# Sums of phi(k) v as four 32 by 33 products on TensorE's column groups instead of one of 128 by 129

## The reference

```
qkv = conv1x1(x); agg = conv1x1_grouped(conv5x5_depthwise(qkv))
ms  = concat([qkv, agg]) -> 64 heads of (q, k, v), each 8 dims, 4096 positions
q, k = relu(q), relu(k);  v = [v, 1]            # 9th column of ones
kv  = einsum('bgnd,bgne->bgde', k, v)            # per head: 8 x 9, summed over n
out = einsum('bgnd,bgde->bgne', q, kv)
out = out[..., :-1] / (out[..., -1:] + 1e-15);  return conv1x1(out)
```

## Time and profile before

| | |
|---|---|
| median of 3 runs | 9206.59 us (9197.57 to 9220.26) |
| the profiled execution's own time | 9182.84 us |
| its span, first to last instruction | 9181.0 us |
| mean granted TensorE clock | 0.917 |
| busy: PE, DVE, POOL, ACT | 84%, 55%, 41%, 38% |

### The profile page before, as it was taken

How to read it: one execution, slowest core, us unless ns; L and a number is a source line. 1 busy time by engine, 2 the same in 40 slices (tenths; PEclk the granted TensorE clock), 3 DMA queues, 4 the chain that set the end, 5 groups by cost and what they waited for, 6 DMA issues and landing times.

```text
span 9181.0 us, 193051 instructions
## 1 busy us (share of the span) xinstructions
PE 7700.7 (84%) x58476; PEld 5340.1 (58%) x58476; DVE 5035.6 (55%) x11563; ACT 3517.2 (38%) x9207; POOL 3781.4 (41%) x10084
## 2 busy tenths in 40 slices
PE   8978799788997889978799788997889978799777
PEld 6645566555665556655566555665556655566555
DVE  3475644756447564475644656447564465644656
ACT  1144621455214552144521445214552145521455
POOL 2335533355333553344533355333553345533454
PEclk9988899888998889988899888998889988999889
DMA  3201122011220112201122011220112201122011
GB/s 99 64 15 26 38 88 64 15 26 38 88 64 15 26 38 87 64 15 27 41 84 64 15 26 38 88 64 15 27 42 83 64 15 27 46 78 64 18 25 54
DMA packets 398691, 431.05 MB, mean 47 GB/s; under 512 B 159184, under 2 KB 355984, under 8 KB 393296
## 3 DMA queue, kind: packets, MB, share of 16 engines
q1 hardware_dynamic: 397648, 418.42, 16.1%
HBM read 102.76 MB, written 67.63 MB: 19 GB/s over the span
## 4 chain that ended last, share of the span: by engine, by line
PE 54%; DVE 23%; issue 7%; DMA 6%; ACT 5%; DVEq 3%; SPq 1%; POOL 1%; POOLq 0%; ACTq 0%
PE PS L621 12%; PE PS L681 7%; DVE arena L1129 5%; PE PS L899 5%; DVE arena L1216 4%; PE PS L768 4%; PE PS L638 3%; PE PS L661 3%; PE PS L864 3%; PE PS L824 3%; PE PS L833 3%; DVE SM L1340 3%; DMA kv_rows<-arena 3%; ACT arena L1073 2%; DVEq L1328 2%
## 5 line engine op out<-in xcount | busy, mean ns | idle before, releaser
L968 ACT ACTIVATE arena<-PS 128x128 f32<-128x128 f32 (+5 forms) x4160 | 1549.5, 398 | 2080.8 <-PE PS L621 595.3
L559 POOL COPY arena<-arena 64x129 f32 x6144 | 1528.8, 291 | 1400.3 <-PE PS L870 1130.3
L483 POOL TENSOR_TENSOR arena<-arena 128x512 f32<-128x512 f32 x768 | 803.9, 1069 | 1493.1 <-PE PS L621 1477.7
L621 PE MATMUL PS<-arena 128*128 128x256 f32 x6144 | 1359.1, 379 | 48.1 <-DMA arena<-arena 43.1
L1129 DVE COPY arena<-PS 64x260 f32<-64x260 f32 (+2 forms) x1272 | 634.1, 514 | 1373.8 <-PE PS L621 527.9
L621 PEld LDWEIGHTS PS<-arena 128*128 128x128 f32 x6144 | 1157.7, 189 | 270.5 <-issue 96.2
L1129 DVE COPY arena<-arena 64x129 f32 x4096 | 845.9, 268 | 409.8 <-PE PS L870 292.5
L804 PE MATMUL PS<-arena 64*64 64x192 f32 x8192 | 710.6, 390 | 252.0 <-POOL arena L559 225.2
L1216 DVE RECIPROCAL arena<-arena 128x512 f32<-128x512 f32 x256 | 857.6, 3350 | 115.6 <-ACT arena L1016 114.1
L489 POOL TENSOR_TENSOR BUF<-BUF,arena 128x512 f32<-128x512 f32 x256 | 358.1, 1399 | 1287.1 <-ACT arena L1004 1287.1
L1340 DVE TENSOR_REDUCE SM<-PS 128x1 f32<-128x384 f32 x1024 | 570.8, 557 | 549.9 <-issue 419.5
(11 more groups left out here) (102 smaller groups left out, 11208.6 us busy)
## 6 DMA issues: line engine op xcount, KB each, us to landing
arena<-arena SPq DMA_DIRECT2D x1024, 128.0 KB, 2.3
arena<-arena SPq DMA_DIRECT2D x768, 144.5 KB
BUF<-in_x SPq DMA_DIRECT2D x18, 2048.0 KB, 11.7
kv_rows<-arena SPq DMA_DIRECT2D x256, 130.0 KB, 3.5
arena<-kv_rows SPq DMA_DIRECT2D x256, 130.0 KB
out<-BUF SPq DMA_DIRECT2D x64, 512.0 KB, 2.6
arena<-in_taps SPq DMA_DIRECT2D x96, 288.0 KB, 3.7
W<-in_w SPq DMA_DIRECT2D x2, 768.0 KB, 5.9
```

What stands on the lines that cost most here:

```text
L483: last = pool.tensor_tensor(o, tap, mix, ALU.mult)
L559: last = pool.tensor_copy(G[p % GD][0:D, j // 3, j % 3, :], KVB[0:D, bass.ds(off, KVW)])
L621: last = nc.tensor.matmul(bank(i)[:, a * 256:(a + 1) * 256], lhsT=TW[n % 2][:, a * CH + k * P:a * CH + (k + 1) * P], rhs=src[:, k // 2:k / ...
L968: return nc.scalar.activation(o, i, ACT.Copy)
```

## The change

The product of 128 by 129 becomes four, one for each group of 32 channels: 32 columns of weights (one group's phi(k)) and 33 columns of moving data (that group's v and a column of ones). Each writes the 32 PSUM partitions of its own group, columns 0 to 32, of the bank that took the whole before. What falls away are products of one group's k with another group's v, which the mask set to zero. `VTS` holds eight runs of 33 for two of 129; the copy into it and the memset of ones follow. `kv_weights` reads the 32 columns four times over, once for each block of columns of the mask.

```diff
-        VTS = [l0.take(2 * (P + 1)) for _ in range(2)]
+        VTS = [l0.take(2 * 4 * 33) for _ in range(2)]
...
-                        pool.memset(VTS[s].rearrange("p (u n) -> p u n", u=2)[:, :, P:P + 1], 1.0).then_inc(s_zero, 1)
+                        pool.memset(VTS[s].rearrange("p (u n) -> p u n", n=33)[:, :, 32:33], 1.0).then_inc(s_zero, 1)
...
                                 for u in range(2):
-                                    last = nc.tensor.matmul(PS[:, 4 + src, 0:P + 1],
-                                                            lhsT=KTS[t % 2][:, u * P:(u + 1) * P],
-                                                            rhs=VTS[t % 2][:, u * (P + 1):(u + 1) * (P + 1)],
-                                                            start=(t == 0 and u == 0),
-                                                            stop=(t == n_items - 1 and u == 1))
+                                    for quarter in range(4):
+                                        rows = slice(32 * quarter, 32 * (quarter + 1))
+                                        at = 4 * u + quarter
+                                        last = nc.tensor.matmul(PS[rows, 4 + src, 0:33],
+                                                                lhsT=KTS[t % 2][:, 32 * at:32 * (at + 1)],
+                                                                rhs=VTS[t % 2][:, 33 * at:33 * (at + 1)],
+                                                                start=(t == 0 and u == 0),
+                                                                stop=(t == n_items - 1 and u == 1))
...
-                    copy(VTS[t % 2].rearrange("p (u n) -> p u n", u=2)[:, :, 0:P],
-                         PS[:, i % 4, 2 * P:4 * P].rearrange("p (u n) -> p u n", u=2)).then_inc(s_free[e], 1)
+                    copy(VTS[t % 2].rearrange("p (u n) -> p u n", n=33)[:, :, 0:32],
+                         PS[:, i % 4, 2 * P:4 * P].rearrange("p (u n) -> p u n", n=32)).then_inc(s_free[e], 1)
...
-                            order.after(nc.vector.tensor_copy(KSUM[:, src:src + 1], PS[:, 4 + src, P:P + 1]))
-                            nc.vector.tensor_tensor(WN[src], PS[:, 4 + src, 0:P], same_head, ALU.mult)
+                            order.after(nc.vector.tensor_copy(KSUM[:, src:src + 1], PS[:, 4 + src, 32:33]))
+                            quarters = lambda tile: tile.rearrange("p (a n) -> p a n", a=4)
+                            nc.vector.tensor_tensor(quarters(WN[src]),
+                                                    PS[:, 4 + src, 0:32].unsqueeze(1).broadcast_to([P, 4, 32]),
+                                                    quarters(same_head), ALU.mult)
```

More of the change, by code:

```diff
@@ L120, in build @@
         BUF = [sb(f"BUF{k}", [P, KT, L]) for k in range(2)]
-        ARENA = 31098
+        ARENA = 31110
         arena = sb("arena", [P, ARENA])
```

## The result

The changed kernel took 9127.70 us (median of 4 runs, 9122.07 to 9140.56) where the kernel before, beside it, took 9204.66: ratio 0.9924, 95% interval 0.9899 to 0.9948. Timed again in five rounds (first experiment) the ratio was 0.9941, 0.9922 to 0.9959, and once more, beside a third kernel, 0.9950, 0.9933 to 0.9966. So it is faster by some 0.5 to 0.6%, about 50 us; the 77 us between the first medians didn't come again. The two profiled executions are 50.4 us apart (9182.84 and 9132.41). One of ten executions of the run with narrow products in the raw stages alone took 14918 us, in a slow state, and stands outside every ratio.

The account below looks back on a forecast made before the run. PE was taken as busiest (84% of the span), with DVE's way from transpose to product deciding kv_sums pairs; 46 us from steady pairs and 6 at the ends, -52 us, against the median 9206.59 gave 9155, range 9130 to 9290.

Parts of the forecast that it names:

- Four groups at once: Products in kv_sums: 16 narrow passes in four rounds of 0.032 us on four column groups; block 0.27 us for 0.54.
- Drain and opened load: Switching between transposes and column groups in kv_sums: 0.09 us drain, and 0.05 more for the first transpose's weights.
- What decides the pair: Two steady kv_sums items: DVE's cycle of 1.13 + 0.27 + 0.38 = 1.78 us decides, against PE's 1.70; 2.00 before.
- The sum: All kv_sums stages: 208 steady pairs x 0.22 = 46 us, and 6 at the 32 ends, together -52 us.
- The rule against it: Narrow products: each matmul carries some 60 cycles, so 0.40 us for the block's streams, a pair of 2.20, 9253 us.
- Two groups as a limit: Rival at the products: only two column groups run at once, block 0.38, pair 1.92, -18 us, 9189; chance 0.15.
- A least time a pass: Rival at the 16 passes: 0.029 us each whatever the width, 9280 us, chance 0.14; worse form 9505, chance 0.05.
- The clock: Rival: narrow passes may not hold full clock; +65 us (9270) if aggregated stages stay low, +250 in all; chance 0.10.
- What I had put at nothing: Copy in runs of 32, memsets of ones, kv_weights' reads, and conv after raw stages: no cost, no gain given back.

Follow-up runs that it names:

- first experiment: The changed kernel timed again in five rounds with no edit, against the kernel before: ratio 0.9941 (0.9922 to 0.9959).
- third kernel: Changed kernel plus three unused products of 128 by 512 in PE's wait in each aggregated stage, on the same chip: 9111.54 us, 0.9928 to the kernel before.
- run on one group: Changed kernel with all narrow passes on the first column group, except in a stage's last item: ratio 1.0087 to the kernel before, +80 us.
- two filled kernels: Changed kernel and kernel before, each with three unused products in PE's wait in each aggregated stage: ratios 0.9924 and 0.9972.
- layout alone: Changed kernel's layout (VTS in runs of 33, copy, memset, mask) with one product of 128 by 132: ratio 1.0009 to the kernel before.
- raw alone: Changed kernel with narrow products in the raw stages only, one product of 128 by 132 in the aggregated ones: ratio 0.9968 to the kernel before.

## Why the prediction was right, and where it wasn't

The forecast was 9155 us, 52 us less; measured are 50 in the profiled pair and 54 in the five rounds, and the forecast's ratio, 9155 to 9206.59 or 0.9944, lies in each of the three intervals. Point by point:

*Four groups at once.* Right, and shown by the run on one group. The bet was on a combination that the trace of before didn't hold; L864's two groups at full rate and L804's four starts in 0.03 us were the right neighbours. Forecast 0.27 for the block, measured 0.26. (L864's pairs lie 0.002 to 0.003 above their streams, not 0.004, by which the block would have come to 0.26 or 0.27.) What sets a round I had named only in part: I counted the streams, but halving these left the rounds as they were, and only halving the weights as well ended them. So the loads of 32 columns suffice for 0.032, and that the number held is in part luck.

*Drain and opened load.* Right: 444.50 to 444.71 is 0.21 for a forecast of 0.20, and the transposes after a block are 0.38 from first to last (444.97 to 445.35), as forecast.

*What decides the pair.* Right: DVE's 1.13 stays, the pair is 1.77 for a forecast 1.78.

*The sum.* Its size fits in part by luck, because errors cancel. A raw stage gained 2.19 for 8 x 0.22 + 0.13 = 1.89. The eight pairs, from the second item's products to the last one's, gave the 1.76 forecast. But the first item, which I didn't count, gave 0.13, and the last products gave 0.30 from first to last start (0.44 before, 0.14 now) where I had 0.13. An aggregated stage gained 1.2 for 5 x 0.22 + 0.25 = 1.35. In the two filled kernels, at an even clock, it is 1.9: seven pairs gain there, and not five. In the changed kernel as it is, the first eight items together gain nothing, and half clock lasts 6.8 us for 3.8; only the last four pairs and the last products gain. So I had the number of pairs too low and the clock's part at nothing, and together they are small: 5 us too little for the raw stages, 2 too much for the aggregated ones.

*The rule against it.* The estimate from the Trainium skill's sentence in "TensorEngine Tiling (Array Packing)", Instruction Overhead (60 cycles a matmul, 9253 us) did not come true: the passes start 7 ns apart on average within a round, not 25. On one and the same group they were 0.033 apart, which doesn't speak against the rule, and there the change lost. So in these runs the rule's 60 cycles can stand for passes on one column group, and not for passes that go to different groups in turn.

*Rivals.* Two groups as a limit: out, since four were seen at once; as a kernel of its own it is level. A least time a pass: if there is one, it is some 6.4 ns, too small to matter at 32 columns. The clock: I gave it 0.10 as an event that decides (its sum, 80 x 1.2 - 28, is 68 and not 65, which changes nothing). It came true in a small way: no raw stage fell from full clock, yet after the wait in the aggregated stages half clock lasted 6.8 us for 3.8. Filling the wait took nearly all of it away in both kernels. That products on several groups go with the longer half clock is supported by the run with narrow products in the raw stages alone, by the run on one group and by the table, in one to three executions of each kernel. Why they should delay the clock's return is not settled by these runs.

*What I had put at nothing.* Copy, memsets and `kv_weights` cost nothing that can be seen. Conv follows a raw stage's last products directly, 0.13 to 0.18 us from start to start (0.11 before): nothing gave the gain back but these 0.05 us a stage.

## What to carry to other kernels

When a product's result is wanted only in blocks along its diagonal, four narrow products on the four column groups can take the place of one wide product, provided that consecutive ones go to different groups: here 16 passes in rounds of 0.032 us for 4 of 0.11. The price here was a drain of some 0.09 us each way and a load in the open, so that it has to pay per visit. Read which joint of the loop ends last before counting: here DVE's emptying caps the gain at 0.23 of 0.56 us a pair (twice 0.54 - 0.26). And where PE waits for a few us ahead of such passes, read the granted clock behind the wait: filling it with unused products gave some 28 us more by the medians, 30 by the stages.

Not tried: two engines emptying one item, which would have them read one PSUM bank at the same time, and a third pair of `KTS` and `VTS`, which takes 520 more columns of the arena. Both would attack DVE's 1.13 us.

## What the runs showed of the hardware

The regularity of the starts was new to me: on four column groups of full height 16 fp32 passes with their loads of weights start within 138 ns, and with halved weights and columns within 109, from the fifth on some 6.4 ns apart. On one group the same passes start 33 ns apart.

And PE's time at half clock (1.2 GHz) in an aggregated stage without filling, whose longest wait of PE is 0.9 to 3.3 us, was on average 3.6 to 4.7 us with wide products (before, layout alone, raw alone), 4.7 with narrow ones on one group, 6.8 with products on two groups and 6.4 to 8.1 on four (halved columns and weights included). With the wait filled it was 0.2 to 0.6. These are means of 16 stages in one execution of each kernel, and what brings the difference about stays open.
